# Row maxima read over two PSUM banks at a time, with the projection and the turned maxima inside the bank rings

## What is computed

```python
def _L0_xattn_ref(query, key, value, Wq, bq, Wk, bk, Wv, bv, Wo, bo):
    q = proj(query, Wq, bq); k = proj(key, Wk, bk); v = proj(value, Wv, bv)
    q = q * cos + rotate_half(q) * sin
    k = k * cos + rotate_half(k) * sin
    attn = jnp.einsum('bhqd,bhkd->bhqk', q, k) * scale
    attn_w = jax.nn.softmax(attn, axis=-1)
    out = jnp.einsum('bhqk,bhkd->bhqd', attn_w, v)
    out = out.transpose(0, 2, 1, 3).reshape(B, S, D)
    return jnp.einsum('bsd,ed->bse', out, Wo) + bo

x = x + jnp.tanh(g_xattn[0]) * xattn(_layernorm(x), ctx_1024, ctx_1024, ...)
x = x + jnp.tanh(g_ffn[0]) * ffn(_layernorm(x), ...)      # weights and activations rounded to 8 bits
```

## Time and profile before

| | |
|---|---|
| median of three runs | 639.18 us |
| the profiled execution | 641.87 us, its span 640.0 us, 1.87 us around it |
| TensorE busy over the span | 572.1 us (89%) |
| VectorE busy | 549.8 us (86%), of it 319.3 us in the 512 row maxima of L864, 677 ns each |
| ScalarE busy | 441.5 us (69%), of it 278.7 us in the 512 exponentials of L805 |
| GpSimd busy | 264.2 us (41%) |
| the granted TensorE clock, in 40 slices of 16 us | 9899999569999979999999999999999997799889 |

### The profile page before, as it was taken

How to read it: one execution, slowest core, us unless ns; L and a number is a source line. 1 busy time by engine, 2 the same in 40 slices (tenths; PEclk the granted TensorE clock), 3 DMA queues, 4 the chain that set the end, 5 groups by cost and what they waited for, 6 DMA issues and landing times. The chain is left out here.

```text
span 640.0 us, 18888 instructions
## 1 busy us (share of the span) xinstructions
PE 572.1 (89%) x6473; PEld 275.9 (43%) x6478; DVE 549.8 (86%) x935; ACT 441.5 (69%) x886; POOL 264.2 (41%) x372
## 2 busy tenths in 40 slices
PE   3999997999899989999999999999999983878485
PEld 1655554233344434444444444444444421433164
DVE  2799999899999869899899899899799757498878
ACT  2666766247677757787787687687687691688694
POOL 3898897601233434214214214214214202699400
PEclk9899999569999979999999999999999997799889
DMA  8559876522422224223223224224211000000025
GB/s 284 191 164 293 240 205 192 149 52 62 81 62 53 72 46 85 50 63 87 50 60 86 53 57 86 55 54 85 60 53 48 3 2 2 0 2 0 0 89 176
DMA packets 61256, 55.21 MB, mean 86 GB/s; under 512 B 11040, under 2 KB 58784, under 8 KB 61216
## 3 DMA queue, kind: packets, MB, share of 16 engines
q1 hardware_dynamic: 61216, 54.70, 33.0%
HBM read 37.62 MB, written 16.78 MB: 85 GB/s over the span
## 5 line engine op out<-in xcount | busy, mean ns | idle before, releaser
L864 DVE TENSOR_REDUCE negm<-mx_ps 128x1 f32<-128x512 f32 x512 | 319.3, 677 | 33.9 <-PE mx_ps L682 31.2
L805 ACT ACTIVATE prob<-st_ps 128x512 f32<-128x512 f32 x512 | 278.7, 597 | 98.3 <-PE st_ps L673 96.5
L682 PE MATMUL mx_ps<-k,q 96*32 96x512 bf16 x2048 | 221.4, 401 | 4.7 <-PEq L311 3.1
L673 PE MATMUL st_ps<-q,k 98*32 98x512 bf16 x2048 | 214.5, 386 | 4.8 <-ACT prob L805 3.5
L695 PE MATMUL pv_ps<-prob,v_u 128*32 128x512 f32 x1024 | 135.7, 598 | 8.6 <-DVE turned L873 5.8
L682 PEld LDWEIGHTS mx_ps<-k,q 96*32 96x32 bf16 x2048 | 64.0, 97 | 107.9 <-DVE negm L864 72.6
L673 PEld LDWEIGHTS st_ps<-q,k 98*32 98x32 bf16 x2048 | 68.8, 97 | 83.2 <-ACT prob L805 49.7
L1031 POOL TENSOR_TENSOR msplit<-negm,onesf 128x16 bf16<-128x16 f32 x32 | 7.1, 221 | 148.2 <-DVE negm L864 137.5
L1051 POOL TENSOR_TENSOR normal<-turned,recip 128x256 f32<-128x256 f32 x32 | 19.9, 621 | 99.5 <-DVE recip L879 99.5
L695 PEld LDWEIGHTS pv_ps<-prob,v_u 128*32 128x32 f32 x1024 | 32.5, 110 | 34.1 <-ACT prob L805 21.7
L298 POOL TENSOR_TENSOR parts<-work 128x512 bf16<-128x512 f32 x32 | 38.3, 1206 | 7.5 <-DVE work L286 6.0
(11 more groups left out here) (129 smaller groups left out, 729.0 us busy)
## 6 DMA issues: line engine op xcount, KB each, us to landing
qk_parts<-parts SPq DMA_DIRECT2D x96, 128.0 KB, 2.7
k<-qk_parts SPq DMA_DIRECT2D x192, 64.0 KB, 2.7
q<-qk_parts SPq DMA_DIRECT2D x192, 64.0 KB, 2.9
ctx<-in_ctxT SPq DMA_DIRECT2D x8, 512.0 KB, 4.4
X<-in_x SPq DMA_DIRECT2D x8, 512.0 KB, 7.9
out<-X SPq DMA_DIRECT2D x7, 512.0 KB, 2.9
q<-mrow SPq DMA_DIRECT2D x64, 4.0 KB, 2.5
wf<-in_w_down SPq DMA_DIRECT2D x1, 704.0 KB, 4.4
```

What stands on the lines that cost most here:

```text
L673: last = nc.tensor.matmul(st_ps[bank(i)][lo:lo + COLS, :], k6[g][:, h, kt * P + lo:kt * P + lo + COLS], q6[g][:, h, :], start=True, stop=True)
L682: last = nc.tensor.matmul(mx_ps[bank(i)][lo:lo + COLS, :], q6[g][0:ROWS, h, qt * P + lo:qt * P + lo + COLS], k6[g][0:ROWS, h, :], start=Tr ...
L805: nc.scalar.activation(prob[kt % 2][:, h, :], st_ps[bank(HPU * kt + h)][:], ACT.Exp, scale=SCALE).then_inc(exp_done, 1)
L864: nc.vector.tensor_reduce(negm[g % 2][:, h * TPB + qt:h * TPB + qt + 1], mx_ps[bank(TPB * h + qt)][:], op=ALU.max, axis=AX.X, negate=True) ...
```

## The change

The six banks of `mx_ps`, `misc_ps` and `st_ps` that were three, one and three become two pairs `mx_ps` (four banks) and three `st_ps`; `misc_ps` is gone.

- Two query groups fill the two banks of a pair, and one VectorE instruction takes both maxima (1024 elements in, 2 out). In a step TensorE's order is now score 0, pair, score 1, score 2, pair, score 3, `weigh`; it was score, query, score, query, score, query, `weigh`, score, query.
- The turned maxima take a place in the ring of `st_ps`, after the fourth score group (ring place 4 of 17), and `take_max` on ScalarE stands at the end of step 0, after its last exponential.
- `project` writes into the first bank of a pair that has been read. The pairs of steps 2 and 3 of g = 1 and g = 2 change places for it; the second pair of step 2 waits for `residual`, which now stands ahead of both maxima of step 2.
- The bias product of the prologue goes into `st_ps[2]`. The turned weights of the last units use the two banks of `mx_ps[0]`, the last two projections the banks of `mx_ps[1]`.

```diff
-        mx_ps = [ps(psB, f"mx_ps{i}", [P, S]) for i in range(2)]
-        misc_ps = ps(psB, "misc_ps", [P, 512])
+        mx_ps = [ps(psB, f"mx_ps{i}", [P, 2, S]) for i in range(2)]
         pv_ps = ps(psB, "pv_ps", [P, S])
-        mx_ps.append(ps(psB, "mx_ps2", [P, S]))
...
-        def bank(i):
-            return i % 3 if i < 15 else 1
-
-        def wait_bank_read(eng, read, u, i):
-
-            n = 16 * u + i
-            back = {0: 4, 1: 2, 2: 4, 15: 2}.get(i, 3)
-            if not isinstance(n, int) or n >= back:
-                eng.wait_ge(read, n - back + 1)
+        TURN_SLOT = HPU
+        PROJ_PAIR = (0, 1)
+
+        def slot(i):
+
+            return i if i < TURN_SLOT else i + 1
+
+        def score_bank(i):
+
+            return st_ps[slot(i) % 3]
+
+        turn_bank = st_ps[TURN_SLOT % 3][0:2 * HPU * TPB, 0:P // 2].bitcast(BF16)
+
+        def wait_score_bank(eng, b, g, i):
+
+            n = 16 * (UPB * b + g)
+            if slot(i) == TURN_SLOT + 3 and not (is_last(b) and g == 3):
+                eng.wait_ge(mrow_ready, UPB * b + g + 2)
+            elif i < 3:
+                if not (is_first(b) and g == 0):
+                    eng.wait_ge(exp_done, n - 16 + (14, 15, 13)[i] + 1)
+            else:
+                back = next(j for j in range(16) if slot(j) == slot(i) - 3) if slot(i) != TURN_SLOT + 3 else 1
+                eng.wait_ge(exp_done, n + back + 1)
+
+        def pair_bank(g, kt, j):
+
+            return mx_ps[(2 * kt + j + (g == 2) + (g in (1, 2) and kt >= 2)) % 2]
...
+                def query_scores(b, g, h, j, pair):
+
+                    for qt in (2 * j, 2 * j + 1):
+                        for lo in range(0, P, COLS):
+                            last = nc.tensor.matmul(pair[lo:lo + COLS, qt % 2, :], q6[g][0:ROWS, h, qt * P + lo:qt * P + lo + COLS], k6[g][0:ROWS, h, :],
+                                                    start=True, stop=True)
                     last.then_inc(mx_ready, 1)
+
+                def ahead_scores(b, g, kt, j):
+
+                    mb, mg = (b, g + 2) if g < 2 else (b + 1, g - 2)
+                    n = 8 * (UPB * mb + mg) + 2 * kt + j
+                    if g in (1, 2) and kt == 2 and j == 1:
+                        if not is_first(b):
+                            pe.wait_ge(x1_ready, 2 * (b - 1) + g)
+                    else:
+                        pe.wait_ge(mx_read, n if g in (1, 2) and kt == 2 else n - 1)
+                    query_scores(mb, mg, kt, j, pair_bank(g, kt, j))
...
                     pe.wait_ge(msplit_ready, u + 2)
-                    if is_first(b) or g < 2:
-                        wait_if(pe, mrow_ready, u + 1)
-                    else:
-                        pe.wait_ge(x1_ready, 2 * (b - 1) + g - 1)
+                    if g >= 0:
+                        pe.wait_ge(exp_done, 16 * u + 2)
...
                     if is_tail(b):
-                        dst = tail_ps[hf]
-                        pe.wait_ge(ds_read, 1)
+                        pe.wait_ge(x1_ready, 2 * (B - 1))
+                    elif is_last(b) and hf == 1:
+                        pe.wait_ge(mx_read, 8 * NU)
                     else:
-                        max_taken(b, 1 + hf)
+                        pe.wait_ge(mx_read, 8 * (UPB * b + hf + 3) + 3)
...
                             for h in range(HPU):
-                                if h == HPU - 1:
-                                    if kt:
-                                        weigh(b, g, kt - 1)
-                                    elif not (is_first(b) and g == 0):
-                                        weigh(*((b, g - 1) if g else (b - 1, 3)), 3)
                                 scores(b, g, kt, h)
-                                if ahead:
-                                    query_scores(mb, mg, kt, h)
+                                if ahead and h in (0, 2):
+                                    ahead_scores(b, g, kt, h // 2)
+                            if kt:
+                                weigh(b, g, kt - 1)
+                            elif not (is_first(b) and g == 0):
+                                weigh(*((b, g - 1) if g else (b - 1, 3)), 3)
...
-                            if kt == 1 and not (is_last(b) and g == 3):
+                            exps(b, g, kt, (2, 3))
+                            if kt == 0 and not (is_last(b) and g == 3):
                                 take_max(b, g)
-                            exps(b, g, kt, (2, 3))
...
+                def maxima(b, g, h, j, pair):
+
+                    dve.wait_ge(mx_ready, 8 * (UPB * b + g) + 2 * h + j + 1)
+                    lo = h * TPB + 2 * j
+                    nc.vector.tensor_reduce(negm[g % 2][:, lo:lo + 2], pair[:], op=ALU.max, axis=AX.X, negate=True).then_inc(mx_read, 1)
...
-                            if ahead:
-                                maxima(mb, mg, kt, (0, 1))
-                            if kt == 1 and not (is_first(b) and g == 0):
-                                invert_sums(b, g)
                             if kt == 2 and g in (1, 2) and not is_first(b):
                                 residual(b, g - 1)
                             if ahead:
-                                maxima(mb, mg, kt, (2, 3))
+                                maxima(mb, mg, kt, 0, pair_bank(g, kt, 0))
+                            if kt == 1 and not (is_first(b) and g == 0):
+                                invert_sums(b, g)
+                            if ahead:
+                                maxima(mb, mg, kt, 1, pair_bank(g, kt, 1))
```

More of the change, by code:

```diff
@@ L609, in build, with project_bank @@
         v_blank = sem("v_blank")
[L613 to L629 removed]
+        TURN_SLOT = HPU
[17 more added lines that the diff above has]
+            return mx_ps[(2 * kt + j + (g == 2) + (g in (1, 2) and kt >= 2)) % 2]
+        NWT = 5
+        mx_bf = [mx_ps[0][:, i, :].bitcast(BF16).rearrange("p (n q) -> p n q", q=P) for i in range(2)]
+        ds_ps = mx_ps[0][:, 1, 0:D]
+        wobv_ps = st_ps[2][:, 0:D]
+        def project_bank(b, hf):
+            return mx_ps[1][:, hf, :] if is_tail(b) else mx_ps[PROJ_PAIR[hf]][:, 0, :]
         def is_tail(b):
@@ L663, in _ @@
             def _(pe):
-                def max_taken(b, g):
-                    pe.wait_ge(mrow_ready, UPB * b + g + 2)
                 def scores(b, g, kt, h):
-                    u, i = UPB * b + g, HPU * kt + h
-                    wait_bank_read(pe, exp_done, u, i)
+                    i = HPU * kt + h
+                    wait_score_bank(pe, b, g, i)
                     for lo in range(0, P, COLS):
-                        last = nc.tensor.matmul(st_ps[bank(i)][lo:lo + COLS, :], k6[g][:, h, kt * P + lo:kt * P + lo + COLS], q6[g][:, h, :],
+                        last = nc.tensor.matmul(score_bank(i)[lo:lo + COLS, :], k6[g][:, h, kt * P + lo:kt * P + lo + COLS], q6[g][:, h, :],
                                                 start=True, stop=True)
                     last.then_inc(st_ready, 1)
[L677 to L683, removed]
-                    last.then_inc(mx_ready, 1)
+                def query_scores(b, g, h, j, pair):
[3 more added lines that the diff above has]
+                                                    start=True, stop=True)
+                    last.then_inc(mx_ready, 1)
+                def ahead_scores(b, g, kt, j):
[7 more added lines that the diff above has]
+                    query_scores(mb, mg, kt, j, pair_bank(g, kt, j))
                 def weigh(b, g, kt):
@@ L726, in down_scales @@
                     for c in range(KC):
-                        last = nc.tensor.matmul(mx_ps[1][:, c * P:(c + 1) * P], onesf[:], diag[:, c, :], start=True, stop=True, skip_group_check=True)
+                        last = nc.tensor.matmul(ds_ps[:, c * P:(c + 1) * P], onesf[:], diag[:, c, :], start=True, stop=True, skip_group_check=True)
                     last.then_inc(ds_ready, 1)
                 def project(b, hf):
-                    dst = misc_ps
+                    dst = project_bank(b, hf)
                     pe.wait_ge(attnT_ready, 2 * b)
                     if is_tail(b):
-                        dst = tail_ps[hf]
-                        pe.wait_ge(ds_read, 1)
+                        pe.wait_ge(x1_ready, 2 * (B - 1))
+                    elif is_last(b) and hf == 1:
+                        pe.wait_ge(mx_read, 8 * NU)
                     else:
-                        max_taken(b, 1 + hf)
+                        pe.wait_ge(mx_read, 8 * (UPB * b + hf + 3) + 3)
                     pe.wait_ge(woT_ready, 1)
@@ L778, in _ @@
                     for h in range(HPU):
[L779 to L790, removed]
+                        for j in range(2):
+                            wait_if(pe, mx_read, 8 * g + 2 * h + j - 1)
+                            query_scores(0, g, h, j, mx_ps[j])
+                        if g == 0 and h >= 2:
+                            c = h - 2
+                            if c == 0:
```

(25 more changed lines are left out.)

15 lines of the change are left out of this document (7 added, 8 removed).

## The result

The changed kernel takes 617.85 us (median; 616.9 to 620.49) against 639.43 us before: a ratio of 0.9678, 95% interval 0.9648 to 0.9707. The forecast was 619.5 with a range of 614 to 630. The profiled execution has a span of 616.2 us, 23.8 less than before.

The account below looks back on a forecast made before the run. VectorE was taken as the bound, TensorE within 3%. Gains of 2.4 + 0.6 + 2.6 + 2.4 + 11.5 + 0.5 = 20.0 us cut the span from 640.0 to 620.0; forecast median 619.5, range 614 to 630.

Parts of the forecast that it names:

- VectorE is the bound and its relief brings the gain: Steady batch: VectorE's 44.7 us plus 3.6 of waits make 48.3; its relief is worth at most TensorE's 3.2 of waits.
- A pair costs 1.14: VectorE's maxima: one read of a pair takes 1.14 us against 1.22 for two singles, 2.6 less a batch.
- TensorE's 45.2 plus 0.9 of waits: Steady batch after the change: TensorE's 45.2 us plus waits of 0.5 for pairs and 0.4 for score banks, 46.1.
- The scheme of slacks: Hand schedule of steps of 2.61 us on TensorE, VectorE's slack 0.33 each, giving the waits for pairs and score banks.
- Rival A: A pair costs two singles (1.22) or its handshake eats the relief; VectorE stays the bound: 46.7 a batch, 628 us; chance 0.14.
- Rival D: Copy of the turned maxima over 0.3 us late stops exponentials and scores; 0.3 in each of 31 units, 629; chance 0.08.
- Rival C: Coarser waits of two pairs make TensorE's clock fall, 2.9 us each; two a steady batch give 648, slower; chance 0.06.
- Batch 1, 2.4 forecast: From batch 1's g = 1: two projection units 1.4, g = 3 (GpSimd's weight rounding) 0.4, g = 0 of batch 2 0.6.
- Batch 0, 2.6 forecast: Four units of batches 0 and 1, VectorE's throughout because of weight maxima: 4 x 8 x 0.08 = 2.6 us gained.
- Prologue and first unit, 3.0 forecast: Prologue gains 2.4 us from cheaper maxima and lost idle time; the first unit, half at the low clock, gains 0.6.

Follow-up runs that it names:

- the ring of four: The changed kernel with its four query banks filled and read one by one, a maximum of 512 elements each: 620.98 us, ratio 0.9709.
- single reads and the means first: The changed kernel with four single query banks, read one by one, and GpSimd's means of the new X before its weight rounding: 614.98 us, ratio 0.9664.

## Why the prediction was right, and where not

- *VectorE is the bound and its relief brings the gain.* This is the step that was wrong, though the number came out. VectorE's 44.7 us a batch was read off a spacing of 0.611. The single starts in the trace say otherwise: in the kernel before as in the ring of four, one maximum follows another after 0.598, and the nine of the earlier trace rows hold one distance of 0.692, a wait too short to be listed. With 0.598 the same sum gives 43.9. In the ring of four VectorE was busy for 43.7 us in a batch of 45.80: nearly full, but not what set the length. The number of banks, the places of the projection and of the turned maxima, and the place of `weigh` held TensorE and VectorE to each other. The fourth bank with the new places gains 0.4 (48.01), `weigh` alone loses 0.6 (48.94), and all together gain 2.6 without a cheaper read. The relief is not worthless everywhere: with `weigh` ahead, the pairs read at once take 1.0 less than the ring of four (47.03 against 48.01), and with pairs two reads cost 0.80. With `weigh` behind, the ring of four and the cheaper read are two ways to the same 45.80.
- *A pair costs 1.14.* Right: two pairs in a row mostly start 1.13 to 1.14 apart (303.64 2.35 x2 gives 2.35 - 1.21 = 1.14). The term that was off is the single maximum. Two of them are 1.20 and not 1.22, so a pair saves 0.05 to 0.06 and not 0.08, or 1.7 a batch and not 2.6.
- *TensorE's 45.2 plus 0.9 of waits.* Measured 45.80, so 0.6 of waits. The scheme of slacks held place by place: the second pair of step 2 of g = 3 waits 0.15 (forecast 0.34), the first score of a unit behind an x1_spread 0.12 and that of step 1 0.11 (0.14 each), a projection 0.07 (0.1), the copy nothing. This arithmetic, and not the diagnosis above, carried the forecast. That TensorE is now the bound fits with these few gaps and with two kernels of different VectorE work that both take 45.80. No run relieved TensorE, so what would come next is open.
- *Rival A* (46.7, 628): the run with two reads of a pair gave 46.60 and 627.86. So the prediction itself gave the cheaper read only 0.6 of a batch's 2.3, and the run gives it 0.80 of 2.6.
- *Rival D.* The place of the copy matters as told: 1.1 a unit where it comes half a step late. Where the loss begins was not measured.
- *Rival C.* No second low clock, and 1.00 in the windows of all steady batches; the one behind the stop in batch 1 was even missing from the changed kernel's profile, which the prediction had not foreseen.
- *Batch 1, 2.4 forecast, 5.05 measured.* The mean clock of that stretch rose to 1.00. Before, groups after the stop stood 0.43 apart for 6 us; after, they were back at 0.22 within a microsecond. The stop itself was still 2.70. Other kernels with such a stop showed either, so I take it for luck of the execution and not for the change; as every kernel has one profile, that is not shown. With the 0.9 of the first block there are 3.8 us in the 23.8 of the profiled run that the change did not bring or need not have. What is left is 20.0, the forecast's own sum.
- *Batch 0, 2.6 forecast, 1.6 measured.* The 2.6 took VectorE for the bound throughout and 0.08 a pair. With single reads and the means first VectorE is busy in all 46.53 us of the stretch; with pairs it is busy 44.8 of 45.81, that is 1.7 less, and waits 0.4 in step 2 of two units. So the cheaper reads take 0.05 a pair off VectorE's work, and 1.0 of the 1.7 turns into idle time: VectorE alone no longer sets the time there.
- *Prologue and first unit, 3.0 forecast.* From the first maximum to `turn_out` of g = 1 is 37.03 before and 34.06 after: 3.0.

## What to carry to other kernels

Where two engines are both over 90% busy and pass buffers to each other, the buffers can be the bound although a sum over one engine seems to account for the time. Before an instruction is made cheaper, ask how the same list runs with one buffer more and with a burst moved. Test a change of several parts by crossing them: here the fourth bank with its new places gained 0.4 by itself, the moved `weigh` lost 0.6, and both together gained 2.6. Read an engine's cost from single starts: a mean over a merged row hides short waits, here 0.013 us for each of 64 instructions, or about 0.8 a batch. An instruction that frees a buffer belongs where its engine would idle otherwise: half a step later, the copy cost more than the whole change brought.

## What was not expected of the hardware

Matmuls of 32 columns for different heads ran side by side, in fp32 too: eight took 0.86 us and so did four. After the stop in batch 1 the granted clock fell to half for 3 to 7 us in eight profiles (stops of 1.82 to 3.18 us) and stayed in three (2.46, 2.59 and 2.70 us), so in these runs the length of the stop alone does not tell which it will be.
